# Routed expert tiles: turning the gathered rows by SBUF transfers and 32x32 blocks on VectorE in place of TensorE transposes

## The chip, the core and the metric

One core of one Trainium2 chip runs one program. The metric is device time in microseconds (us). The engines are called PE (TensorE; PEld is its weight load), DVE (VectorE), ACT (ScalarE), POOL (GpSimd) and SP (SyncE, which only issues transfers). A q behind a name (SPq) is that engine's instruction sequencer.

## The reference, cut to what matters

```
y      = clip((x * styles) @ weight.T * dcoefs + bias)       # 8192 tokens of 512 columns
shared = silu(y @ sh_gate_w) * (y @ sh_up_w) @ sh_down_w     # 1024 hidden
topk_idx, w = _route(y, router_w, e_bias)                    # 8 of 64 experts for each token
g = ragged_dot(y[tok], gate_w, group_sizes)                  # 512 -> 256 for each token's expert
u = ragged_dot(y[tok], up_w, group_sizes)
o = ragged_dot(silu(g) * u, down_w, group_sizes)             # 256 -> 512
out = x + shared + scatter_add(o * w)
```

Everything is float32. Each product is made of three fp32r matmuls: both operands are split in a high and a low part, and high by high, high by low and low by high are added up in PSUM.

## The kernel before, in words

**Dense stage (up to about 1396 us).** 16 blocks of 512 tokens: y is made in columns, turned back to rows and stored in `y_rows` in DRAM by `y_row` (line 624), the shared network is computed and stored in `out`, and the router writes for each expert a list of slots (row of y, weight) in `slot_list`. A table of tiles is made at the end: each tile has 128 rows of one expert.

**Routed stage (from about 1396 us).** 532 tiles of 128 rows (133 turns of `UN` = 4 tiles). Every engine runs its own `step(g, u)` for tile j = 4g + u in program order; semaphores join them:

- SP (lines 1101 to 1162): `step` of n loads tile n's list (`load_list`, line 1106; it waits until the scatter of tile n - 16 has landed, line 1112), and then, if tile n - 2 is the first one of an expert, loads that expert's weights (`weights`, line 1116): three transfers, 1.57 MB. `weights` waits until the weights before have landed (lines 1127, 1129). There are 29 such loads.
- POOL (from line 1164): `step(j)` waits until PE has turned tile j (`pe_x`, line 1190), gathers the 128 rows of tile j + 4 from `y_rows` into `x_rows` (line 1169), waits for `act_do`, reads a field of the table, and adds the result of tile j - 3 to `out` (`scatter`, line 1185). For a flagged tile (the first of an expert, and filling tiles) it first waits until all scatters before have landed.
- PE (from line 1214): `step(j)` is `gate_up(j)` (12 matmuls, line 1232), `turn_x(j + 2)` (4 transposes of the gathered rows into the PSUM banks `b_x`, line 1223), `turn_h(j - 1)` (2 transposes, line 1241), `down(j - 2)` (6 matmuls, line 1250).
- ACT (from line 1286): `weigh(j - 3)` (line 1315), `start_weights(j + 2)` if an expert begins there, `silu(j)` (line 1300), `x_high(j + 2)` (line 1294), `h_high(j - 1)`, `end_weights`.
- DVE (from line 1377): `weights_low` parts 1 and 2 of tile j + 1's expert if it begins there, `hidden(j)` (line 1398), `x_low(j + 2)`, `rows_from(j + 6)` (line 1387, the row numbers for the gather), `h_low(j - 1)`, `weights_low` part 0 of tile j + 2's expert. The subtractions all go through the helper `sub_exact` and so show line 30.

`gate_up(j)` waits for `x_low(j)`; `turn_h(j)` for `hidden(j)`; `down(j - 1)` for `h_low(j - 1)`; `hidden(j)` for `silu(j)`, and that for `gate_up(j)`. `weigh(j)` may write its buffer once the scatter of tile j - 4 has landed. `x_rows` has 4 buffers, `b_x` and `x_h`/`x_l` have 2.

The order of the experts puts a small one between two large ones: 9 times one tile of a small expert stands ahead of a large one, so that two loads of weights follow each other with one tile's list between them; twice two lists stand between the two loads, and the remaining 6 loads behind the first one of the stage lie further apart or close such a wider group.

Of the kernel before, what the change touches and what calls it, by code (L numbers as in the profile page):

```python
# [16 lines left out]
P = 128  # L17
# [15 lines left out]
def build(nc, x, cond, cw, cbias, aff_w, aff_b, router_w, e_bias, gate_w, up_w, down_w,  # L33
# [18 lines left out]
    UN = 4  # L52
# [4 lines left out]
    FLD = 7  # L57

# [11 lines left out]
    with top:  # L70
# [224 lines left out]
        with ExitStack() as tmp:  # L295
# [311 lines left out]
            def _(act):  # L607
# [16 lines left out]
                def y_row(q, t):  # L624
                    act.wait_ge(pe_ty, TT * q + t + 1)
                    if some(16 * (TT // 2 * q + t // 2)):
                        act.wait_ge(y_st[t % 2], 16 * (TT // 2 * q + t // 2))
                    nc.scalar.copy(yrow[:, t % 2, :], misc[(t + 1) % 2][:]).then_inc(act_yrow, 1)
# [391 lines left out]
        with ExitStack() as tmp:  # L1020
# [13 lines left out]
            xg = [sb(f"x_rows{n}", [P, C], F32, LINE) for n in range(UN)]  # L1034
            xp = [sb("x_h", [P, 2, KC, P], F32R, LINE), sb("x_l", [P, 2, KC, P], F32R, LINE)]
            sg = sb("e_sg", [P, 2, H])
            hf = sb("e_hf", [P, 2, H], F32, LINE)
            ident_r = sb("ident_r", [P, P], F32R, LINE)
# [3 lines left out]
            b_gu, b_x, b_h, b_o = bank[0:2], bank[2:4], bank[4:6], bank[6:8]  # L1042
# [10 lines left out]
            words, words_chain, ident_ok = sem("words"), sem("words_chain"), sem("ident_ok")  # L1053
            pe_x, act_x, dve_x = sem("pe_x"), sem("act_x"), sem("dve_x")
# [9 lines left out]
            AHEAD = 2  # L1064
# [37 lines left out]
            def _(sp):  # L1102
# [32 lines left out]

                def step(g, u):
                    n = g * UN + u
                    load_list(n, u, g)
                    if not isinstance(n, int) or n >= AHEAD:
                        weights(n - AHEAD)  # L1140

# [7 lines left out]
                with sp.Fori(LISTS // UN, NTURN + 1) as g:  # L1149
                    with sp.If(last_turn >= g - 1):  # L1150
                        for u in range(UN):
                            step(g, u)
                for u in range(2):
                    sp.wait_ge(list_ld[u], 16 * last_turn + 32)
                    sp.nop(nofuse=True)
                    sp.wait_ge(added[u], 16 * last_turn)
                    sp.nop(nofuse=True)
                    off = field(sp, UN * last_turn + 2 * UN + u, 0, LROWS - P)
                    sp.dma_start(entry(UN * last_turn + 2 * UN + u, 0, 2), slots[bass.ds(off, P), :]).then_inc(list_ld[u], 16)
                for u in range(UN):  # L1160
                    sp.wait_ge(list_ld[u], 16 * last_turn + (48 if u < 2 else 32))
# [3 lines left out]
            def _(pool):  # L1165
                def gather(g, u):
                    pool.wait_ge(dve_from, g * UN + u + 1)
                    pool.nop(nofuse=True)
                    nc.gpsimd.indirect_dma_start(xg[u][:], None, y_rows,  # L1169
# [18 lines left out]
                def step(g, u):  # L1188
                    j = g * UN + u
                    pool.wait_ge(pe_x, j + 1)  # L1190
                    gather(g + 1, u)
# [4 lines left out]
                for u in range(UN):  # L1196
                    gather(0, u)
# [11 lines left out]
                for u in range(UN):  # L1209
                    pool.wait_ge(x_ld[u], 16 * last_turn + 32)  # L1210
# [4 lines left out]
            def _(pe):  # L1215
                pe.wait_ge(tab_ld, 16)
                pe.sem_inc(pe_do, 1)

                def turn_x(j, u, g):

                    pe.wait_ge(x_ld[u], 16 * (g + 1))
                    for k in range(KC):
                        last = nc.tensor.transpose(b_x[u % 2][:, k * P:(k + 1) * P].bitcast(F32R),  # L1223
                                                   xg[u][:, k * P:(k + 1) * P].bitcast(F32R), ident_r[:])
                    last.then_inc(pe_x, 1)
# [29 lines left out]
                def step(g, u, turn):  # L1255
# [5 lines left out]
                    turn_x(j + 2, (u + 2) % UN, g + 1 if u >= UN - 2 else g)  # L1261
# [5 lines left out]
                pe.wait_ge(ident_ok, 1)  # L1267
                pe.wait_ge(words, 1)
                turn_x(0, 0, 0)
                turn_x(1, 1, 0)  # L1270
# [16 lines left out]
            def _(act):  # L1287
                act.wait_ge(tab_ld, 16)

                def x_high(j, u):  # L1290
                    act.wait_ge(pe_x, j + 1)
                    if not isinstance(j, int) or j >= 2:
                        act.wait_ge(pe_gu, j - 1)
                    nc.scalar.copy(xp[0][:, u % 2, :, :].rearrange("p k t -> p (k t)"), b_x[u % 2][:]).then_inc(act_x, 1)  # L1294
# [83 lines left out]
            def _(dve):  # L1378
                dve.wait_ge(tab_ld, 16)
                dve.sem_inc(split, SPLIT_0)  # L1380
                nc.vector.tensor_copy(ident_r[:], ident[:]).then_inc(ident_ok, 1)
# [118 lines left out]
```

## Time and profile before

| | us |
|---|---|
| median of 3 runs | 3939.05 |
| lowest, highest of the 3 | 3933.24, 15044.9 |
| the profiled execution's own time | 3924.35 |
| its span | 3922.7 |
| mean granted TensorE clock over the span | 0.988 |

The profile is of one execution. Its span runs from the first to the last instruction, and its own time is 1.65 us more than the span. Both are some 15 us (0.4%) below the median of the runs.

### The profile page before, as it was taken

How to read it: one execution, taken by the hardware profiler on the slowest of the kernel's cores; microseconds unless marked ns; L12 is line 12 of the kernel's file. 1: busy time of each engine (PE TensorE's matmuls, PEld its weight loads, DVE VectorE, ACT ScalarE, POOL GpSimd, SP SyncE). 2: the span in 40 equal slices, each digit the busy share in tenths (PEclk: the TensorE clock that was granted, in tenths of full speed). 3: DMA queues.
4: the chain of work that ended last, by engine and by line, in shares of the span. 5: the costliest groups of instructions: out<-in, count | busy, mean ns of one | idle time of the engine just before them, and what ended most of it. 6: DMA issues, size and time to landing. Idle time of an engine off the chain costs nothing.

```text
span 3922.7 us, 92670 instructions
## 1 busy us (share of the span) xinstructions
PE 3834.2 (98%) x19160; PEld 3179.8 (81%) x19161; DVE 1691.2 (43%) x4076; ACT 1507.8 (38%) x3339; POOL 1921.1 (49%) x1598
## 2 busy tenths in 40 slices
PE   6999999999999969999999999999999999999998
PEld 5888888888888858888888888888888888888886
DVE  4655555555555633333333333333333333333343
ACT  3222222222222224444444444444444444444444
POOL 1353343333343425555555555555555555555554
PEclk7999999999999989999999999999999999999999
DMA  5121121121122136666666676667676666777766
GB/s 183 44 66 44 44 59 51 49 60 44 50 61 44 33 88 113 113 139 120 113 144 115 114 144 113 143 115 145 113 144 113 144 144 113 145 144 145 146 144 128
DMA packets 296940, 409.20 MB, mean 104 GB/s; under 512 B 116137, under 2 KB 151345, under 8 KB 296817
## 3 DMA queue, kind: packets, MB, share of 16 engines
q0 software_dynamic: 135872, 280.60, 38.2%
q1 hardware_dynamic: 160946, 127.03, 12.3%
q8 instruction: 70, 1.15, 0.2%
q14 instruction: 52, 0.43, 0.1%
HBM read 228.29 MB, written 179.19 MB: 104 GB/s over the span
## 4 chain that ended last, share of the span: by engine, by line
PE 62%; issue 1%; DVE 0%; ACT 0%; ACTq 0%; DVEq 0%; SPq 0%; DMA 0%; POOL 0%; POOLq 0%
PE bank L1232 36%; PE bank L1250 18%; PE bank L1223 4%; PE bank L1241 3%; DVE w_dn_l L30 0%; ACTq L1068 0%; SPq L1068 0%; ACT w_dn_h L1320 0%; DVEq L1079 0%; DMA trow<-tile_table 0%; ACT w_gu_h L1320 0%; ACT x_h L1294 0%; DVE turns L1444 0%; DVE w_gu_l L30 0%; ACTq L1320 0%
## 5 line engine op out<-in xcount | busy, mean ns | idle before, releaser
L1185 POOL DMA_INDIRECT out_dram<-o_rows,to_row x532 | 862.0, 1620 | 930.6 <-issue 750.2
L425 POOL DMA_INDIRECT slot_list<-ent,pos x512 | 504.5, 985 | 822.3 <-PE bank L451 377.0
L1398 DVE TENSOR_TENSOR e_hf<-bank,e_sg 128x256 f32<-128x256 f32 x532 | 225.6, 424 | 1554.6 <-ACT e_sg L1300 1162.6
L1232 PE MATMUL bank<-w_gu_h,x_h 128*128 x2128 | 831.5, 391 | 10.1 <-DVE x_l L30 5.1
L1232 PE MATMUL bank<-w_gu_h,x_l 128*128 x2128 | 830.9, 390 | 0.0
L1232 PE MATMUL bank<-w_gu_l,x_h 128*128 x2128 | 828.9, 390 | 0.0
L1169 POOL DMA_INDIRECT x_rows<-y_rows,from_row x536 | 535.5, 999 | 213.3 <-issue 129.2
L1300 ACT ACTIVATE e_sg<-bank 128x256 f32<-128x256 f32 x532 | 204.4, 384 | 833.5 <-PE bank L1232 831.8
L1232 PEld LDWEIGHTS bank<-w_gu_h,x_h 128*128 128x128 f32 x2128 | 399.9, 188 | 102.1 <-issue 18.9
L1232 PEld LDWEIGHTS bank<-w_gu_h,x_l 128*128 128x128 f32 x2128 | 400.1, 188 | 83.5
L1232 PEld LDWEIGHTS bank<-w_gu_l,x_h 128*128 128x128 f32 x2128 | 400.0, 188 | 82.3
L1250 PE MATMUL bank<-w_dn_h,e_h_h 128*128 x1064 | 463.0, 435 | 0.5 <-issue 0.5
L1250 PE MATMUL bank<-w_dn_l,e_h_h 128*128 x1064 | 418.2, 393 | 0.0
L1250 PE MATMUL bank<-w_dn_h,e_h_l 128*128 x1064 | 414.8, 390 | 0.0
L30 DVE TENSOR_TENSOR x_l<-bank,x_h 128x512 fp32r<-128x512 f32 x534 | 368.9, 691 | 28.8
L1315 ACT ACTIVATE o_rows<-bank,lists 128x512 f32<-128x512 f32 x532 | 367.4, 691 | 0.0
L1223 PEld LDWEIGHTS bank<-ident_r,x_rows 128*128 128x128 f32 x2136 | 241.5, 141 | 95.0 <-issue 25.5
L1294 ACT CAST x_h<-bank 128x512 fp32r<-128x512 f32 x534 | 313.5, 587 | 0.0
L1314 ACT COPY to_row<-lists 128x1 int32 (+1 forms) x532 | 102.4, 192 | 519.2 <-PE bank L1250 510.5
L1223 PE MATMUL bank<-ident_r,x_rows 128*128 128x128 f32 x2136 | 246.0, 239 | 25.8 <-DVE turns L1450 24.9
L652 ACT ACTIVATE sg<-bank 128x512 f32<-128x512 f32 x128 | 76.6, 598 | 426.4 <-PE bank L451 426.4
L1250 PEld LDWEIGHTS bank<-w_dn_h,e_h_l 128*128 128x128 f32 x1064 | 200.5, 188 | 44.7
(244 smaller groups left out, 5988.9 us busy)
## 6 DMA issues: line engine op xcount, KB each, us to landing
xin<-in_x_dram SPq DMA_DIRECT2D x16, 1024.0 KB, 5.8
y_rows<-yrow SPq DMA_DIRECT2D x64, 256.0 KB, 3.1
stage_d<-in_x_dram SPq DMA_DIRECT2D x16, 1024.0 KB
out_dram<-stage_d SPq DMA_DIRECT2D x16, 1024.0 KB, 8.4
raw_gu<-in_L_ffn_gate_w_dram SPq DMA_DIRECT2D x29, 512.0 KB
raw_gu<-in_L_ffn_up_w_dram SPq DMA_DIRECT2D x29, 512.0 KB
raw_d<-in_L_ffn_down_w_dram SPq DMA_DIRECT2D x29, 512.0 KB
lists<-slot_list SPq DMA_DIRECT2D x538, 1.0 KB
```

The lines of the kernel that those rows point to most:

```text
L30: return nc.vector.tensor_tensor(out, full, high.bitcast(F32), ALU.subtract)
L425: nc.gpsimd.indirect_dma_start(slots, bass.IndirectOffsetOnAxis(ap=pos[v][:, t, k:k + 1], axis=0), ent[v][:, t, k, :], None).then_inc(scat ...
L1169: nc.gpsimd.indirect_dma_start(xg[u][:], None, y_rows, bass.IndirectOffsetOnAxis(ap=from_row[u][:].bitcast(U32), axis=0)).then_inc(x_ld[u] ...
L1185: nc.gpsimd.indirect_dma_start(out, bass.IndirectOffsetOnAxis(ap=to_row[u][:].bitcast(U32), axis=0), og[u][:], None, compute_op=ALU.add).t ...
L1223: last = nc.tensor.transpose(b_x[u % 2][:, k * P:(k + 1) * P].bitcast(F32R), xg[u][:, k * P:(k + 1) * P].bitcast(F32R), ident_r[:])
L1232: last = nc.tensor.matmul(b_gu[u % 2][:], xp[a][:, u % 2, k, :], wgu[b][:, bass.ds(place, 1), k, :].rearrange("p a n -> p (a n)"), start=( ...
L1241: last = nc.tensor.transpose(b_h[u % 2][:, k * P:(k + 1) * P], hf[:, u % 2, k * P:(k + 1) * P], ident[:])
L1250: last = nc.tensor.matmul(b_o[u % 2][:], hp[a][:, u % 2, k, :], wdn[b][:, bass.ds(place, 1), k, :].rearrange("p a n -> p (a n)"), start=(k ...
L1294: nc.scalar.copy(xp[0][:, u % 2, :, :].rearrange("p k t -> p (k t)"), b_x[u % 2][:]).then_inc(act_x, 1)
L1300: nc.scalar.activation(sg[:, u % 2, :], b_gu[u % 2][:, 0:H], ACT.Silu).then_inc(act_gu, 1)
L1315: nc.scalar.activation(og[u][:], b_o[u % 2][:], ACT.Copy, scale=entry(j, 1, 2).bitcast(F32)).then_inc(act_do, 1)
L1398: nc.vector.tensor_tensor(hf[:, u % 2, :], b_gu[u % 2][:, H:2 * H], sg[:, u % 2, :], ALU.mult).then_inc(dve_gu, 1)
```

## The change

`turn_x` leaves PE. The gathered rows take another way into columns:

- `y_row` stores each row of y with its 512 columns in another order: column 128m + 32a + r goes to place 128a + 32m + r. The rest of the dense stage is as before.
- SP gets `spread(j)`: once the gather of tile j has landed and DVE has turned tile j - 2, four transfers inside SBUF bring quarter a of the 128 rows (128 partitions of 512 bytes) to the 32 partitions from 32a on (2048 bytes each) of `x_split`, which has 2 buffers.
- DVE gets `turn_x(j)`: one 32x32 block transpose of 128x512 elements from `x_split` into the new SBUF tile `x_cols`.
- `x_high` and `x_low` read `x_cols` in SBUF instead of the PSUM bank `b_x`.
- The gathers run two tiles further ahead (tile j + 6 in POOL's step j, ahead of it a wait for the spread of tile j + 2 in place of the wait for `pe_x`), `rows_from` one tile further, DVE's `turn_x` stands one tile ahead of `x_low`. SP's loop runs one turn longer, in place of the two list loads behind it.

```diff
@@ y_row
-                    nc.scalar.copy(yrow[:, t % 2, :], misc[(t + 1) % 2][:]).then_inc(act_yrow, 1)
+                    nc.scalar.copy(yrow[:, t % 2, :].rearrange("p (a m r) -> p m a r", a=QD, m=KC),
+                                   misc[(t + 1) % 2][:].rearrange("p (m a r) -> p m a r", m=KC, a=QD)).then_inc(act_yrow, 1)
@@ tiles
+            x_split = [sb(f"x_split{n}", [P, QD, KC * SQ]) for n in range(2)]
+            x_cols = sb("x_cols", [P, 2, KC, P])
-            ident_r = sb("ident_r", [P, P], F32R, LINE)
-            AHEAD = 2
+            AHEAD, BEHIND = 2, 5
@@ SP
+                def spread(j, u, g):
+
+                    sp.wait_ge(x_ld[u], 16 * (g + 1))
+                    sp.nop(nofuse=True)
+                    if not isinstance(j, int) or j >= 2:
+                        sp.wait_ge(dve_turned, j - 1)
+                        sp.nop(nofuse=True)
+                    for a in range(QD):
+                        sp.dma_start(x_split[u % 2][a * SQ:(a + 1) * SQ, :, :],
+                                     xg[u][:, a * P:(a + 1) * P]).then_inc(x_moved[u], 16)
+
                 def step(g, u):
                     n = g * UN + u
                     load_list(n, u, g)
+                    if not isinstance(n, int) or n >= BEHIND:
+                        spread(n - BEHIND, (u - BEHIND) % UN, g + (u - BEHIND) // UN)
                     if not isinstance(n, int) or n >= AHEAD:
                         weights(n - AHEAD)
-                with sp.Fori(LISTS // UN, NTURN + 1) as g:
-                    with sp.If(last_turn >= g - 1):
+                with sp.Fori(LISTS // UN, NTURN + 2) as g:
+                    with sp.If(last_turn >= g - 2):
@@ POOL
                 def gather(g, u):
                     pool.wait_ge(dve_from, g * UN + u + 1)
                     pool.nop(nofuse=True)
+                    if some(g):
+                        pool.wait_ge(x_moved[u], 16 * QD * g)
+                        pool.nop(nofuse=True)
@@ POOL step
-                    pool.wait_ge(pe_x, j + 1)
-                    gather(g + 1, u)
+                    gather(g + 1 + (u + 2) // UN, (u + 2) % UN)
@@ PE
-                def turn_x(j, u, g):
-
-                    pe.wait_ge(x_ld[u], 16 * (g + 1))
-                    for k in range(KC):
-                        last = nc.tensor.transpose(b_x[u % 2][:, k * P:(k + 1) * P].bitcast(F32R),
-                                                   xg[u][:, k * P:(k + 1) * P].bitcast(F32R), ident_r[:])
-                    last.then_inc(pe_x, 1)
@@ PE step
                     gate_up(j, u, place)
-                    turn_x(j + 2, (u + 2) % UN, g + 1 if u >= UN - 2 else g)
@@ ACT x_high
-                    act.wait_ge(pe_x, j + 1)
+                    act.wait_ge(dve_turned, j + 1)
-                    nc.scalar.copy(xp[0][:, u % 2, :, :].rearrange("p k t -> p (k t)"), b_x[u % 2][:]).then_inc(act_x, 1)
+                    nc.scalar.copy(xp[0][:, u % 2, :, :], x_cols[:, u % 2, :, :]).then_inc(act_x, 1)
@@ DVE
-                    sub_exact(nc, xp[1][:, u % 2, :, :].rearrange("p k t -> p (k t)"), b_x[u % 2][:],
-                              xp[0][:, u % 2, :, :].rearrange("p k t -> p (k t)")).then_inc(dve_x, 1)
+                    sub_exact(nc, xp[1][:, u % 2, :, :], x_cols[:, u % 2, :, :], xp[0][:, u % 2, :, :]).then_inc(dve_x, 1)
+
+                def turn_x(j, u, g):
+                    dve.wait_ge(x_moved[u], 16 * QD * (g + 1))
+                    if not isinstance(j, int) or j >= 2:
+                        dve.wait_ge(act_x, j - 1)
+                        dve.wait_ge(dve_x, j - 1)
+                    nc.vector.transpose(x_cols[:, u % 2, :, :].rearrange("p k (c i) -> p k i c", i=QD),
+                                        x_split[u % 2][:].rearrange("p i (k r) -> p k i r", r=SQ)).then_inc(dve_turned, 1)
@@ DVE step
                     hidden(j, u)
+                    turn_x(j + 3, (u + 3) % UN, g + (u + 3) // UN)
                     x_low(j + 2, (u + 2) % UN)
-                    rows_from(j + 2 + UN, (u + 2) % UN, g + 2 if u >= UN - 2 else g + 1)
+                    rows_from(j + 3 + UN, (u + 3) % UN, g + 1 + (u + 3) // UN)
@@ DVE ahead of the loop
+                for u in range(3):
+                    rows_from(UN + u, u, 1)
+                for u in range(2):
+                    turn_x(u, u, 0)
                 for u in range(2):
                     x_low(u, u)
-                    rows_from(UN + u, u, 1)
+                turn_x(2, 2, 0)
```

## Rows read from the trace of the kernel before

**Rows 1.** The page's chain that ended last, shares of the span by line.

```profile
PE bank L1232 36%; PE bank L1250 18%; PE bank L1223 4%; PE bank L1241 3%; DVE w_dn_l L30 0%; ACTq L1068 0%; SPq L1068 0%; ACT w_dn_h L1320 0%; DVEq L1079 0%; DMA trow<-tile_table 0%; ACT w_gu_h L1320 0%; ACT x_h L1294 0%; DVE turns L1444 0%; DVE w_gu_l L30 0%; ACTq L1320 0%
```

**Rows 2.** Windows: length; busy PE, PEld, DVE, ACT, POOL (count); PE clock; DMA share; GB/s.

```profile
1400.00:1425.00 25.00, 6.21 (x19) 4.91 (x20) 8.75 (x20) 3.91 (x5) 5.73 (x6) 0.50 0.45 127
1420.00:3923.00 2503.00, 2479.90 (x12768) 2062.70 (x12768) 892.92 (x2214) 1121.74 (x2744) 1393.67 (x1064) 1.00 0.67 129
```

**Rows 3.** Timeline of one tile: start us, length us, engine, line, what.

```profile
2401.15 0.39 PE L1232 MATMUL bank<-w_gu_h,x_h 128*128 x1
...
2401.76 0.69 ACT L1315 ACTIVATE o_rows<-bank,lists 128x512 f32<-128x512 f32 x1
...
2403.88 0.46 PE L1223 MATMUL bank<-ident_r,x_rows 128*128 128x128 f32 x4
2404.03 1.59 POOL L1185 DMA_INDIRECT out_dram<-o_rows,to_row  x1 [1.88 <-issue]
...
2404.17 0.41 PE L1241 MATMUL bank<-ident,e_hf 128*128 128x128 f32 x2
2404.33 0.48 PE L1250 MATMUL bank<-w_dn_h,e_h_h 128*128 x1
...
2404.99 0.69 DVE L30 TENSOR_TENSOR x_l<-bank,x_h 128x512 fp32r<-128x512 f32 x1
...
2405.66 0.41 DVE L30 TENSOR_TENSOR e_h_l<-bank,e_h_h 128x256 fp32r<-128x256 f32 x1
2405.80 0.39 PE L1232 MATMUL bank<-w_gu_h,x_h 128*128 x1
2405.93 0.98 POOL L1169 DMA_INDIRECT x_rows<-y_rows,from_row  x1 [0.30 <-DVE from_row L1387]
```

**Rows 4.** Timeline of SP where two loads of weights follow each other.

```profile
2502.59 0.34 SPq L1114 DMA_DIRECT2D lists<-slot_list  x1
2506.32 0.40 SPq L1131 DMA_DIRECT2D raw_gu<-in_L_ffn_gate_w_dram  x1
...
2507.51 0.38 SPq L1133 DMA_DIRECT2D raw_d<-in_L_ffn_down_w_dram  x1
2509.17 0.36 SPq L1114 DMA_DIRECT2D lists<-slot_list  x1
2515.73 0.40 SPq L1131 DMA_DIRECT2D raw_gu<-in_L_ffn_gate_w_dram  x1
```

**Rows 5.** Waits of SP in 2500 to 2520: us in total, times, longest.

```profile
SPq L1129 <- DMA raw_d<-in_L_ffn_down_w_dram: 3.1, 1, 3.1
```

**Rows 6.** SP's issues and table reads, all of them: ns min/median/max.

```profile
L1114 SPq DMA_DIRECT2D lists<-slot_list x536: 345/351/369, 1403.8 to 3862.1; - x179
L1131 SPq DMA_DIRECT2D raw_gu<-in_L_ffn_gate_w_dram x29: 392/403/423, 1401.5 to 3859.1; - x29
L1068 SPq TENSOR_LOAD <-trow x1131: 260/268/1018, 1399.0 to 3888.3; - x189
```

**Rows 7.** Windows, ahead of a load of weights and in it (columns as in rows 2).

```profile
2490.00:2506.00 16.00, 16.00 (x83) 13.31 (x82) 4.51 (x12) 6.39 (x16) 8.14 (x7) 1.00 0.68 115
2507.60:2515.20 7.60, 7.60 (x38) 6.29 (x38) 2.06 (x7) 2.77 (x7) 3.65 (x4) 1.00 1.03 297
```

**Rows 8.** The page's queue of SP's transfers: packets, MB, share of 16 engines.

```profile
q1 hardware_dynamic: 160946, 127.03, 12.3%
```

**Rows 9.** Groups of DVE and its release of PE, 1500 to 3850 and 1450 to 3890.

```profile
L30 DVE TENSOR_TENSOR w_gu_l<-raw_gu,w_gu_h x52 | 61.6, 1219 | 3.6 <-issue 3.3
L30 DVE TENSOR_TENSOR w_dn_l<-raw_d,w_dn_h x26 | 31.6, 1216 | 0.0
PE bank L1232 <- DVE w_dn_l L30: 3.9, 9, 0.6
```

**Rows 10.** Timeline: POOL beside DVE's work on weights, and POOL when it is late.

```profile
1729.69 1.22 DVE L30 TENSOR_TENSOR w_dn_l<-raw_d,w_dn_h  x1
...
1730.23 2.15 POOL L1185 DMA_INDIRECT out_dram<-o_rows,to_row  x1 [2.96 <-PE bank L1223]
...
1764.72 0.98 POOL L1169 DMA_INDIRECT x_rows<-y_rows,from_row  x1 [0.30 <-issue]
1766.01 1.59 POOL L1185 DMA_INDIRECT out_dram<-o_rows,to_row  x1 [0.30 <-issue]
...
1769.19 1.59 POOL L1185 DMA_INDIRECT out_dram<-o_rows,to_row  x1 [0.30 <-issue]
```

More of the change, by code:

```diff
@@ L57, in build @@
     FLD = 7
+    SQ = 32
+    QD = P // SQ
+    assert KC * SQ == P
     xf = x.rearrange("b l c -> (b l) c")
@@ L1037, in build @@
             hf = sb("e_hf", [P, 2, H], F32, LINE)
-            ident_r = sb("ident_r", [P, P], F32R, LINE)
             hp = [sb("e_h_h", [P, 2, KH, P], F32R, LINE), sb("e_h_l", [P, 2, KH, P], F32R, LINE)]
             og = [sb(f"o_rows{n}", [P, C]) for n in range(UN)]
-            b_gu, b_x, b_h, b_o = bank[0:2], bank[2:4], bank[4:6], bank[6:8]
+            b_gu, b_h, b_o = bank[0:2], bank[4:6], bank[6:8]
             tab_ld = sem("tab_ld")
@@ L1052, in build @@
             w_high = sem("w_high")
-            words, words_chain, ident_ok = sem("words"), sem("words_chain"), sem("ident_ok")
-            pe_x, act_x, dve_x = sem("pe_x"), sem("act_x"), sem("dve_x")
+            words, words_chain = sem("words"), sem("words_chain")
+            x_moved = [sem(f"x_moved{n}") for n in range(UN)]
+            dve_turned, act_x, dve_x = sem("dve_turned"), sem("act_x"), sem("dve_x")
             pe_gu, act_gu, dve_gu = sem("pe_gu"), sem("act_gu"), sem("dve_gu")
@@ L1148, in _ @@
                 last_turn = field(sp, 0, 5, NTURN - 1)
-                with sp.Fori(LISTS // UN, NTURN + 1) as g:
-                    with sp.If(last_turn >= g - 1):
+                with sp.Fori(LISTS // UN, NTURN + 2) as g:
+                    with sp.If(last_turn >= g - 2):
                         for u in range(UN):
                             step(g, u)
[L1153 to L1159, printed above, removed]
                 for u in range(UN):
-                    sp.wait_ge(list_ld[u], 16 * last_turn + (48 if u < 2 else 32))
+                    sp.wait_ge(list_ld[u], 16 * last_turn + 48)
                     sp.nop(nofuse=True)
@@ L1195, in _ @@
                 pool.wait_ge(tab_ld, 16)
-                for u in range(UN):
-                    gather(0, u)
+                for n in range(UN + 2):
+                    gather(n // UN, n % UN)
                 for u in range(UN):
@@ L1209, in _ @@
                 for u in range(UN):
-                    pool.wait_ge(x_ld[u], 16 * last_turn + 32)
+                    pool.wait_ge(x_ld[u], 16 * last_turn + (48 if u < 2 else 32))
                 for u in range(UN):
@@ L1265, in step @@
                         down(j - 2, (u - 2) % UN, turn.place(u - 2))
-                pe.wait_ge(ident_ok, 1)
                 pe.wait_ge(words, 1)
-                turn_x(0, 0, 0)
-                turn_x(1, 1, 0)
                 for g in range(2):
```

1 line of the change is left out of this document (removed).

## The prediction

> **What bounds the kernel now.** I read the chain that ended last first. PE's lines make nearly all of it, and the transposes of the gathered rows (L1223) have 4% of the span, some 157 us [rows 1]. The window over the routed stage then says that PE is busy 2479.90 of 2503 us at clock 1.00, with DVE at 893, ACT at 1122 and POOL at 1394 us [rows 2]. The timeline of one tile gives the pace: `gate_up` starts at 2401.15 and the next one at 2405.80, so 4.65 us a tile without a gap: 2.73 for the 12 matmuls, 0.29 for `turn_x` (2403.88 to 2404.17), 0.16 for `turn_h`, 1.47 for `down` [rows 3]. PE is the bound, and what comes off it counts only until something else is late. So the other readings are of the engines and the queue that take the work over: SP's timeline at a load of weights [rows 4, 5], the cost of SP's instructions [rows 6], the DMA share in such a load [rows 7], and the groups and the timeline of DVE and POOL [rows 9, 10].
>
> **The change part by part.** I sum against the profiled execution (span 3922.7 us, own time 3924.35); the median of the runs is 3939.05, 15 us more, and I carry the difference over to it.
>
> *PE.* 532 times 0.29 us: -154 us. That is the row's gap between two starts and not the 0.46 us of busy time. The new pace would be 4.36 us.
>
> *DVE, in an ordinary tile.* It gets one transpose of 128x512 more. No row shows one. Below, the subtraction of the same shape takes 0.69 us [rows 3]; above, I take twice that, 1.38, if it goes at half rate. I take 0.69. `x_low` from SBUF I cost at nothing: `w_dn_l`, with all operands in SBUF, takes 1.216 us for 1024 elements a partition [rows 9], which lies on one line with 0.69 for 512. The deadline: `gate_up`'s last matmul ends at about 2404.03 and `h_low(j - 1)` at 2406.07, 2.04 later, 2.8 with the transpose. `down(j - 1)`, which needs it, would start at 2404.33 - 0.29 + 4.36, 4.4 later [rows 3]. 1.5 us are left, so nothing is paid. At 1.38 there are 0.8 left, and still nothing is.
>
> *DVE, where an expert begins.* `weights_low` adds 2 times 1.22 and 1.22, 3.65 us [rows 9]. Now PE waits 9 times for `w_dn_l`, 3.9 us in all [rows 9], at the 9 places where two loads follow each other: there DVE is just late. At these, two or three transposes more (1.4 to 2.1 us) meet a PE that is 0.6 to 0.9 us earlier: about 2.2 us each, +20 us. From both sides: 0, if ACT's and DVE's start moves ahead, and 45 us with transposes of 1.38.
>
> *ACT.* `x_high` reads SBUF instead of PSUM; `silu` and `h_high` stay as they are. 0, with 0.05 us each way, hidden as ACT is busy 45% [rows 2]. The copy in `y_row` moves the same 512 elements in runs of 32; its 64 copies lie beside a PE-bound dense stage: 0.
>
> *SP.* Its step has two table reads (0.268 each and as much again around them), one issue (0.351) and waits [rows 6]. From the end of the weights' last issue (2507.89) to the start of the next list's issue are 1.28 us, and from a list's issue to the first issue of weights, with three reads on the way, 3.73 [rows 4]. I work out 2.3 to 2.4 us for an ordinary step (1.28 + 0.35 + one read and its branch at 0.7). `spread` adds two waits with their nops (0.25) and four issues. Each lasts between 0.351 (one row of descriptors a partition) and 0.403 (the weights' shape) [rows 6], 0.04 between them: 1.6 to 1.8. The new step is 4.2 to 4.4 us, and I take 4.3: just under PE's 4.36. SP becomes the second bound, which is a rival below. A step with weights is 6.58 (2502.59 to 2509.17) [rows 4], 4.25 more than an ordinary one.
>
> *The spread's way through the queue.* 256 KB a tile in pieces of 512 bytes. No row shows a transfer inside SBUF. Queue q1's mean packet costs 0.123 * 3922.7 * 16 / 160946 = 48 ns for 789 bytes [rows 8]: by bytes 1.0 us a tile on all 16 engines, by packets 1.5. DMA share would go from 0.67 to 0.67 * 4.65 / 4.36 + 1.0 / 4.36 = 0.94 (1.06 by packets, which would be too much; 0.71 if it cost nothing). I take 1.0: bytes, since both sides lie in SBUF. In an ordinary tile it is in time. Call T the moment at which DVE has turned tile k - 2 and `spread(k)` may be issued. It is 1.65 us behind the end of `gate_up(k - 5)`, as the transpose takes the place of today's `x_low` (2404.99) and lasts 0.69; DVE wants tile k 0.95 us behind the end of `gate_up(k - 3)`, which is T + 8.0, and PE feels it at T + 9.5. Issues until T + 1.8 and a landing some 3 us later leave 4 us: nothing is paid.
>
> *Behind a load of weights* it is paid. The weights go through the same queue as the spreads. A load issued from 2506.32 on has landed at 2515.4 (SP waited 3.1 us for it, up to just ahead of 2515.73), 9.1 us, with the DMA engines at 1.03 [rows 4, 5, 7]. In the new order SP issues `spread(a - 3)` and then the weights of tile a. By its step costs the first of these goes out at T + 1.8 + 3.4, T + 5.2, and the load lands at T + 14.3. `spread(a - 2)`, issued from T + 8 on, stands behind it: T + 16 (1.3 us at the rate of 1.57 MB in 7.6 us, and its receipt), wanted by T + 4.4 + 9.5 = T + 13.9. PE loses 2.2 us. Where the next tile begins an expert too, SP waits for that landing, issues the second load from T + 14.5 on, and `spread(a - 1)` after it lands behind it, at T + 14.5 + 9.1 + 1 + 1.6 = T + 26.2, wanted by T + 8.7 + 9.5 + 2.2 = T + 20.4: 5.8 us more, 8.3 with some jitter. The tile after that is in time. So: 9 close pairs at 8.3 are 75 us, the two wider ones at 5 are 10, 6 other loads at 2.2 are 13: +98 us. From both sides: 0, if transfers don't keep this order, and 160, if the spread goes by packets and half of the stalls are 5 us longer.
>
> *POOL.* Its step ahead of `gather` swaps one wait for another under the scatter (1.59 us), so 0 by itself. Now act_do (end of 2401.76 + 0.69) leads to a scatter 1.58 us later, the scatter and its 0.31 to the next gather, and that ends at 2406.91: 4.46 us [rows 3], more than 4.36. But that isn't a floor. When POOL is late, it repeats each 3.18 us (1766.01 to 1769.19), since it then reads its table under the transfer before [rows 10]. So it falls back by about 1 us and stays there; gathers run a step earlier than needed. Cost 0; from above, the rival.
>
> The trace shows what two SBUF operands on DVE do to POOL: the scatter that starts under `w_dn_l` takes 2.15 instead of 1.59 us [rows 10], about as long as that instruction still ran. `x_low` becomes such an instruction, 0.69 us in each tile: 3.18 + 0.69 = 3.9 us, still under 4.36, so 0. (The Trainium skill, page SBUF — State Buffer, section "SBUF: two separate sides", says that GpSimd shares a port pair with VectorE as an exclusive lock, taken by a VectorE operation in a 2-port mode or with two SBUF inputs. It speaks against moving operands from PSUM to SBUF; the trace agrees for two inputs, and nothing here shows a transpose.)
>
> *Start and end.* Ahead of the first `gate_up` DVE does two transposes and three `rows_from`: +2 us. After the last tile nothing is new.
>
> Sum: -154 + 98 + 20 + 2 = -34 us. From 3924.35 that is 3890, and from the median of 3939 it is **3905 us**, ratio 0.991.
>
> **The rivals.**
>
> *SP is the bound (slower).* SP's chain has its own sum: 532 steps, 29 times 4.25 for weights (123) and 9 times 2 for landings (18). PE's is 532 * 4.36 + 120 = 2440 and that of before 532 * 4.65 = 2474. With a step of 4.3 SP's is 2429 and hidden; from 4.43 on it equals that of before; at 4.6 it is 2588, +114: 4053 us. For it: 4.3 stands on two estimates, and each 0.1 us in the step is 53 us. The table reads go up to 1.018 us [rows 6]. Against it: the issue times are narrow.
>
> *The queue keeps nobody waiting (faster).* If a spread overtakes a load, or lands in time, only 20 + 2 stay: 3939 - 132 = 3807; with the DVE term gone too, 3787. For it: the packets of two queues share the engines, and 4 us of slack are there. Against it: the same queue holds both, and the engines were full for 7.6 us [rows 7].
>
> *POOL is the bound.* If the transpose also shuts POOL out, its step is 3.18 + 1.38 = 4.56 when it meets both: 532 * 4.56 + some 40 for flagged tiles less 2474 is -8: 3931 us.
>
> *The clock.* PE's clock was at 0.50, its level of 1.2 GHz, after 20 us without work, and the first `gate_up` paid some 2.5 us [rows 2]. If each stall of 6 us does that, it is 9 * 2.5, 22 us more: 3927, inside the forecast's own range.
>
> **How the numbers follow.** Forecast with the clock's variant 0.48, queue harmless 0.17, SP 0.23, POOL 0.12. What this measurement can tell from no change is about 2%, so 3860 and 4018. Faster: 0.16 of the second and 0.04 of the first case, 0.20. Slower: 0.20 of SP's and 0.04 of forecast and POOL, 0.24. Same: 0.56. The range takes in the harmless queue and SP at 4.6: 3790 to 4055; the forecast's own is 3850 to 3960.
>
> **What would show it.** Right: the gap between two `gate_up` starts is 4.36 us in the middle of a large expert; PE idles ahead of `down` or `gate_up`, released by DVE's `e_h_l`, some 2 us at each load of weights and 6 at the second one of a close pair, about ten tiles ahead of the expert's first; DVE waits there for the DMA of `x_split`; the transpose lasts 0.69; DMA share is near 0.94. Wrong: SP is never waiting in an ordinary tile and the pace is 4.5 or more; or PE's idle time is under 40 us in all; or POOL's transfers grow beyond 4 us a tile.

## The result and the profile after

The changed kernel takes 4421.07 us (median of 4, 4418.56 to 4432.33), the kernel before 3936.14 beside it: ratio 1.1254, 95% interval 1.1221 to 1.1287. The ratio leaves out the one run of the kernel before that took 15044.9 us, and it isn't the quotient of the two medians, which is 1.123. The forecast was 3905 us and its range ended at 4055. The direction is that of the rival "SP is the bound", and the size is about four times its price of 114 us.

The page after, in this order: busy time by engine, the queue of the hardware transfers, the chain that ended last by engine and by line, and the groups of the new transpose, of the casts and subtractions behind it, and of POOL.

```profile
PE 3841.4 (87%) x17024; PEld 3058.4 (69%) x17025; DVE 2166.1 (49%) x4611; ACT 1526.4 (35%) x3339; POOL 1947.0 (44%) x1600
...
q1 hardware_dynamic: 469394, 267.42, 21.9%
...
SPq 52%; issue 14%; DMA 2%; PE 0%; POOLq 0%; DVE 0%; POOL 0%; DVEq 0%; ACT 0%; ACTq 0%
SPq L1150 28%; SPq L1074 15%; SPq L1120 6%; DMA raw_d<-in_L_ffn_down_w_dram 1%; SPq L1137 1%; SPq L1124 1%; SPq L1147 0%; SPq L1168 0%; DMA x_split<-x_rows 0%; SPq L1118 0%; SPq L1139 0%; DMA out_dram<-o_rows,to_row 0%; SPq L1145 0%; SPq L1148 0%; SPq L1117 0%
...
L1399 DVE STREAM_TRANSPOSE x_cols<-x_split 128x512 f32<-128x512 f32 x535 | 585.4, 1094 | 1057.0 <-DMA x_split<-x_rows 1056.2
...
L1200 POOL DMA_INDIRECT out_dram<-o_rows,to_row x532 | 868.8, 1633 | 386.7 <-issue 372.6
...
L30 DVE TENSOR_TENSOR x_l<-x_cols,x_h 128x512 fp32r<-128x512 f32 x534 | 359.3, 673 | 0.2 <-ACT x_h L1296 0.2
```

Before, PE's lines made the chain [rows 1]. Now 52% of the span is SP's sequencer: 28% the four issues of `spread` (L1150), 15% the reads of the table (L1074), 6% the issue of the lists (L1120). PE has 0%.

The window over the routed stage (columns as in rows 2) answers to [rows 2]:

```profile
1420.00:4419.00 2999.00, 2493.15 (x10640) 1945.79 (x10640) 1365.53 (x2746) 1140.02 (x2744) 1416.49 (x1064) 0.96 0.76 155
```

It is 496 us longer than the stage of before, and no engine is full: PE idles 506 us. Who waits, over 1450 to 4400 us (us in total, times, longest), and the only row that this view has for SP:

```profile
DVE x_cols L1399 <- DMA x_split<-x_rows: 1044.3, 463, 9.7
...
PE bank L1256 <- DVE e_h_l L30: 404.3, 224, 7.8
```

```profile
SPq L1135 <- DMA raw_d<-in_L_ffn_down_w_dram: 2.9, 4, 1.0
```

DVE waits for the spread in 463 tiles, PE for DVE in 224, and SP for next to nothing: 2.9 us in 2950. A queue that never waits, while the engines that need what it issues do, is the likely bound; the experiments below test it. SP's instructions (ns min/median/max, first and last start), and its timeline at the pair of loads of [rows 4]:

```profile
L1150 SPq DMA_DIRECT2D x_split<-x_rows x2140: 556/595/1327, 1408.8 to 4390.3; - x195
```

```profile
L1074 SPq TENSOR_LOAD <-trow x1137: 261/277/1137, 1394.5 to 4391.0; - x190
```

```profile
2501.89 0.35 SPq L1120 DMA_DIRECT2D lists<-slot_list  x1
2502.46 2.57 SPq L1150 DMA_DIRECT2D x_split<-x_rows  x4
2506.95 0.35 SPq L1120 DMA_DIRECT2D lists<-slot_list  x1
2507.52 2.52 SPq L1150 DMA_DIRECT2D x_split<-x_rows  x4
```

An issue of `spread` takes 595 ns, not the 351 to 403 of the issues of before [rows 6], and four of them 2.5 to 2.6 us (mean 2.53), from one start to the next 0.64 to 0.66. The step's mean is (4390.3 - 1408.8) / 535 = 5.57 us; 2.53 of it are the four issues, 3.04 the rest. The starts of two `gate_up` on PE are 5.60 apart in the mean: PE goes at SP's pace.

### The profile page after: what moved, and what is told of

Same layout as the page of the kernel before. It is cut to its first block, busy times and chain, and to the rows that moved or that the text cites. A ratio compares the mean times of both kernels' runs of the same rounds, so it can differ in the third digit from the quotient of the medians.

```text
span 4419.7 us, 93909 instructions
## 1 busy us (share of the span) xinstructions
PE 3841.4 (87%) x17024; PEld 3058.4 (69%) x17025; DVE 2166.1 (49%) x4611; ACT 1526.4 (35%) x3339; POOL 1947.0 (44%) x1600
## 4 chain that ended last, share of the span: by engine, by line
SPq 52%; issue 14%; DMA 2%; PE 0%; POOLq 0%; DVE 0%; POOL 0%; DVEq 0%; ACT 0%; ACTq 0%
SPq L1150 28%; SPq L1074 15%; SPq L1120 6%; DMA raw_d<-in_L_ffn_down_w_dram 1%; SPq L1137 1%; SPq L1124 1%; SPq L1147 0%; SPq L1168 0%; DMA x_split<-x_rows 0%; SPq L1118 0%; SPq L1139 0%; DMA out_dram<-o_rows,to_row 0%; SPq L1145 0%; SPq L1148 0%; SPq L1117 0%
## 5 line engine op out<-in xcount | busy, mean ns | idle before, releaser
L1399 DVE STREAM_TRANSPOSE x_cols<-x_split 128x512 f32<-128x512 f32 x535 | 585.4, 1094 | 1057.0 <-DMA x_split<-x_rows 1056.2
L1184 POOL DMA_INDIRECT x_rows<-y_rows,from_row x538 | 553.6, 1029 | 1233.5 <-DVE from_row L1388 1092.6
L1238 PE MATMUL bank<-w_gu_h,x_h 128*128 x2128 | 865.2, 407 | 115.4 <-issue 45.0
L1238 PE MATMUL bank<-w_gu_l,x_h 128*128 x2128 | 846.9, 398 | 0.0
L1256 PE MATMUL bank<-w_dn_h,e_h_h 128*128 x1064 | 480.2, 451 | 409.6 <-DVE e_h_l L30 404.3
L1256 PEld LDWEIGHTS bank<-w_dn_h,e_h_h 128*128 128x128 f32 x1064 | 205.3, 193 | 494.2 <-issue 468.7
L1256 PE MATMUL bank<-w_dn_h,e_h_l 128*128 x1064 | 434.8, 409 | 0.0
L1296 ACT CAST x_h<-x_cols 128x512 fp32r<-128x512 f32 x534 | 327.6, 614 | 130.8 <-DVE x_cols L1399 128.9
L30 DVE TENSOR_TENSOR x_l<-x_cols,x_h 128x512 fp32r<-128x512 f32 x534 | 359.3, 673 | 0.2 <-ACT x_h L1296 0.2
L1256 PEld LDWEIGHTS bank<-w_dn_l,e_h_h 128*128 128x128 f32 x1064 | 208.5, 196 | 25.9
```

The source lines that it names most:

```text
L30: return nc.vector.tensor_tensor(out, full, high.bitcast(F32), ALU.subtract)
L1184: nc.gpsimd.indirect_dma_start(xg[u][:], None, y_rows, bass.IndirectOffsetOnAxis(ap=from_row[u][:].bitcast(U32), axis=0)).then_inc(x_ld[u] ...
L1238: last = nc.tensor.matmul(b_gu[u % 2][:], xp[a][:, u % 2, k, :], wgu[b][:, bass.ds(place, 1), k, :].rearrange("p a n -> p (a n)"), start=( ...
L1256: last = nc.tensor.matmul(b_o[u % 2][:], hp[a][:, u % 2, k, :], wdn[b][:, bass.ds(place, 1), k, :].rearrange("p a n -> p (a n)"), start=(k ...
L1296: nc.scalar.copy(xp[0][:, u % 2, :, :], x_cols[:, u % 2, :, :]).then_inc(act_x, 1)
L1399: nc.vector.transpose(x_cols[:, u % 2, :, :].rearrange("p k (c i) -> p k i c", i=QD), x_split[u % 2][:].rearrange("p i (k r) -> p k i r", ...
```

## The experiments

Ratios are to the kernel before, timed on the same chip, so they compare across chips and the microseconds less well. The median of the kernel before was 3924.5 beside idle_on_before, half_bytes, two_on_act and words_on_sp, 3960.8 beside idle_flat, act_and_words, weights_in_pieces and idle_turn, and 3960.9 beside the rest. The microseconds that were expected were worked out for the first of these chips. "Period" is the time between two tiles' copies of `to_row` on ACT.

### Is it the instructions on SP?

**idle_on_before.** The kernel before, with `spread`'s four transfers issued into a buffer that nobody reads, and a wait for the transfers of two tiles back. PE still does the transposes.

```diff
+                def idle_spread(j, u, g):
+                    if not isinstance(j, int) or j >= 2:
+                        sp.wait_ge(idle_moved[(u - 2) % UN], 64 * (g + 1 if u >= 2 else g))
+                        sp.nop(nofuse=True)
+                    for a in range(4):
+                        sp.dma_start(idle_to[u % 2][a * 32:(a + 1) * 32, :, :],
+                                     zrow[:, a * P:(a + 1) * P]).then_inc(idle_moved[u], 16)
@@ step
                     load_list(n, u, g)
+                    idle_spread(n, u, g)
```

> The kernel before, to which SP's step gets only the four issues of the change: the same shapes inside SBUF, from a constant tile into a tile that nobody reads, so that no engine waits for them; PE still turns the rows. Theory 1 (the changed kernel is bound by SP's instructions: 5.59 us a tile in its trace, 2.58 of them the four issues): SP's step is 5.3 to 5.6 us here too, the lists come late, and the time is 4300 to 4420 us. Theory 2 (the transfers themselves are late, in the queue or on full DMA engines, and DVE waits for their data): nobody waits for them here, so the time stays under 3980 us. Theory 3 (the DVE transpose and its ports): no transpose here, 3935 us.

Measured: 4372.0 us, ratio 1.1132 (1.1081 to 1.1184), +448 us of the change's +485. The issue, the chain, and who waits longest over 1450 to 4300 us (us in total, times, longest):

```profile
L1143 SPq DMA_DIRECT2D idle_to<-zrow x2144: 547/602/1163, 1400.5 to 4327.9; - x195
```

```profile
SPq 53%; issue 14%; DMA 2%; DVEq 0%; PE 0%; DVE 0%; POOL 0%; POOLq 0%; ACT 0%; ACTq 0%
SPq L1143 29%; SPq L1070 15%; SPq L1116 6%; DMA raw_d<-in_L_ffn_down_w_dram 1%; SPq L1133 1%; SPq L1120 1%; SPq L1161 0%; SPq L1114 0%; SPq L1135 0%; SPq L1140 0%; DMA lists<-slot_list 0%; SPq L1141 0%; SPq L1162 0%; SPq L1113 0%; SPq L1111 0%
```

```profile
DVE from_row L1402 <- DMA lists<-slot_list: 1044.1, 397, 13.6
```

The chain has the shares of the changed kernel's, though no engine waits for these transfers. What is late behind them are the lists, which SP issues too: DVE waits for them 1044.1 us. The loss is SP's time, not the way of the rows.

**half_bytes.** The change, with each transfer moving 256 bytes of each 512 (half of the gathered columns are left out; the rest of `x_split` is zero, by two clears on DVE at the stage's begin).

```diff
-                        sp.dma_start(x_split[u % 2][a * SQ:(a + 1) * SQ, :, :],
-                                     xg[u][:, a * P:(a + 1) * P]).then_inc(x_moved[u], 16)
+                        sp.dma_start(x_split[u % 2][a * SQ:(a + 1) * SQ, :, 0:P // 2],
+                                     xg[u][:, a * P:a * P + P // 2]).then_inc(x_moved[u], 16)
```

> The changed kernel, each of the four transfers with rows of 256 instead of 512 bytes: as many issues and rows, half the bytes. It leaves out half of each gathered row (zeros in its place). Theory 1 (SP's issues): 4390 to 4430 us, no change. Theory 2 (bytes on the DMA engines or in the queue): the share of the DMA engines falls by about a tenth of the span, and the time by over 100 us, to under 4320.

Measured: 4391.67 us, ratio 1.1183, an issue still 595 ns. Half the bytes give back 0.7%, some 28 us, and the intervals of the two ratios (1.1126 to 1.1239 here) overlap. Bytes are not the main cause.

**idle_flat.** As idle_on_before, but from 128 partitions to the same 128 partitions: no change of shape.

```diff
-                        sp.dma_start(idle_to[u % 2][a * 32:(a + 1) * 32, :, :],
+                        sp.dma_start(idle_to[u % 2][:, a, :],
                                      zrow[:, a * P:(a + 1) * P]).then_inc(idle_moved[u], 16)
```

> As idle_on_before, but each of SP's four idle transfers goes from 128 partitions straight to the same 128 partitions (512 bytes each) instead of to 32 of them: as many issues and bytes. If the 0.6 us of an issue come from the change of shape (128 rows into 32 partitions of 4), the issues take 0.35 to 0.40, SP's step is 4.5 to 4.7 us, and the time 3930 to 4020 us. If each transfer inside SBUF costs SP 0.6 us, it is 4350 to 4380 as in idle_on_before.

Measured: 4441.48 us, ratio 1.1201; an issue has a median of 601 ns. The spreading over quadrants is not what makes the issue dear.

**pairs_of_tiles.** Each of the four transfers carries two tiles: half as many issues of `spread` on SP, as many bytes in as many pieces. (To make room the fourth buffer of `o_rows` is the tile of zeros, and the table is read in shorter.)

```diff
-            x_split = [sb(f"x_split{n}", [P, QD, KC * SQ]) for n in range(2)]
+            x_split = [sb(f"x_split{n}", [P, QD, 2, KC * SQ]) for n in range(2)]
@@ spread, in each second step only
                     for a in range(QD):
-                        sp.dma_start(x_split[u % 2][a * SQ:(a + 1) * SQ, :, :],
-                                     xg[u][:, a * P:(a + 1) * P]).then_inc(x_moved[u], 16)
+                        sp.dma_start(x_split[u // 2][a * SQ:(a + 1) * SQ, :, :, :],
+                                     xg2[u // 2][:, :, a * P:(a + 1) * P]).then_inc(x_moved[u // 2], 16)
```

> The four transfers carry two tiles each: as many bytes and pieces as in the change, half as many instructions on SP. Theory 'price per instruction' (0.644 us from one start to the next, whatever it carries): 1.29 us per tile beside 3.01 of the rest, an SP step of 4.3 us, just under PE's 4.37: period median 4.35 to 4.5, ratio to before 1.01 to 1.04. Theory 'price per piece or byte': an issue takes some 1.2 us, the step stays near 5.6 us and the ratio near 1.12.

Measured: 4107.94 us, ratio 1.036 (1.0337 to 1.0383), period median 4.47. Its page, SP's issues (ns min/median/max) and its timeline:

```profile
x_split<-x_rows SPq DMA_DIRECT2D x1072, 128.0 KB
```

```profile
L1152 SPq DMA_DIRECT2D x_split<-x_rows x1072: 17/631/1659, 1438.6 to 4083.8; - x179
```

```profile
2600.92 0.35 SPq L1121 DMA_DIRECT2D lists<-slot_list  x1
2601.79 2.67 SPq L1152 DMA_DIRECT2D x_split<-x_rows  x4
```

Four issues of 128 KB take 2.67 us where four of 64 KB took 2.57: the price is per instruction. It gives back some 350 of the 485 us. The spread now also waits for two gathers, so each pair comes later, and SP itself waits 111.9 us for `x_rows`.

### What taking work off SP is worth

**two_on_act.** Two of the four transfers are issued by ACT, which gets the same two waits ahead of them.

```diff
-                    for a in range(QD):
+                    for a in range(QD // 2):
                         sp.dma_start(...)
@@ ACT, at the start of its step
+                    for a in range(QD // 2, QD):
+                        act.dma_start(x_split[u % 2][a * SQ:(a + 1) * SQ, :, :],
+                                      xg[u][:, a * P:(a + 1) * P]).then_inc(x_moved[u], 16)
```

> The changed kernel, two of the four transfers issued by ACT instead of SP. Same bytes, same shapes, same 16 DMA engines. Theory 1: SP's step falls by half of 2.58 us to 4.3, just under PE's 4.36; what is left is stalls of some 100 us at the loads of weights, so 3900 to 4000 us. ACT has some 2.3 us of work a tile and gets 1.3 more, with no harm. Theory 2: the transfers are as late as before, over 4300 us.

Measured: 4016.56 us, ratio 1.0227 (1.018 to 1.0274), with act_and_words below the best of the change's variants that compute the whole result. The period's median is 4.37, and from one `gate_up` to the next it is 4.35: the pace of 4.36 that the forecast gave PE is real once SP is out of the way. The mean is 4.835: some tiles are far longer.

**words_on_sp.** SP reads a packed word of four tiles where it read the table for each (lists excepted), and the weights go two tiles earlier.

```diff
-                    with sp.If(field(sp, j, 3, 1) > 0):
+                    with sp.If((field(sp, j, 3, 1) if first is None else first) > 0):
@@ step
-                    if not isinstance(n, int) or n >= AHEAD:
-                        weights(n - AHEAD)
+                    if turn is not None:
+                        weights(n, turn.first(u))
```

> The changed kernel, SP learns from a packed word once in four tiles whether an expert begins, as the other engines do, instead of by one table read in each tile. No transfer changes, weights are loaded two tiles earlier. Theory 1: a table read with its register work is 0.75 us of SP's step, less 0.15 for the word, so the step is 5.0 and the time 4080 to 4150 us. Theories 2 and 3: no change, 4400 to 4430 us.

Measured: 4246.78 us, ratio 1.0814, period median 4.96: 534 of SP's 1137 reads are gone and with them 4.4%, some 170 us, where 270 to 340 were expected. By the mean of SP's step, 5.23 us for 5.57, a read and its branch less the word's share are worth 0.34, where I had 0.6.

**act_and_words** has both.

> Both of the reliefs for SP at once: two of the four transfers issued by ACT, and the packed word instead of the table read. SP's step is then some 3.7 us, clear of PE's 4.36. Theory A (what is left at the loads of weights is the queue: spreads wait behind 1.57 MB): the stalls at the loads stay, the time is 3930 to 4000 us, near that of two_on_act. Theory B (what is left is still SP, which falls behind by 4 us in a step with weights and makes it up slowly): the stalls shrink by half, under 3900 us.

Measured: 4061.15 us, ratio 1.0242 (1.0198 to 1.0287), median 4.38, mean 4.836: as two_on_act. SP now waits 259.7 us for DVE (over 1450 to 4000 us):

```profile
SPq L1149 <- DVE x_cols L1423: 259.7, 246, 3.8
```

So SP's time is not what two_on_act still loses; that lies elsewhere.

**pairs_and_words** puts the words on pairs_of_tiles.

> The same with SP's own table reads for the weights taken from a packed word, and the weights two tiles earlier: an SP step of some 3.9 us. If SP is what pairs_of_tiles still loses by, the ratio falls to 1.00 to 1.01; if it is the stalls at the loads of weights (two_on_act and act_and_words stood at 1.023 and 1.024), it stays between 1.01 and 1.03.

Measured: 4068.61 us, ratio 1.0273 (1.0246 to 1.03): three ways of freeing SP end between 1.023 and 1.027.

### What is left once SP is free

SP's timeline in two_on_act at a close pair of loads, and the window on the first of them (columns as in rows 2):

```profile
1686.83 1.23 SPq L1150 DMA_DIRECT2D x_split<-x_rows  x2
1690.82 0.41 SPq L1137 DMA_DIRECT2D raw_gu<-in_L_ffn_gate_w_dram  x1
...
1694.12 1.38 SPq L1150 DMA_DIRECT2D x_split<-x_rows  x2
1700.59 0.39 SPq L1137 DMA_DIRECT2D raw_gu<-in_L_ffn_gate_w_dram  x1
...
1703.93 1.30 SPq L1150 DMA_DIRECT2D x_split<-x_rows  x2
```

```profile
1691.00:1701.00 10.00, 9.29 (x44) 7.35 (x42) 2.76 (x6) 3.53 (x9) 5.16 (x5) 1.00 1.01 267
```

The spreads there are 7.3 and 9.8 us apart instead of 4.4, with the DMA engines at 1.01; two periods of 10.5 and 7.0 us follow at 1695 and 1705. Where these experts' weights are then split on DVE, three more of 6.7, 7.1 and 5.8. I sorted all 531 periods of two_on_act by what lies in them and summed what each is above the median: 100 us in the 47 in which DVE starts a subtraction of weights, 137 us in some 60 others at loads or just behind one, 10 us in the rest. (The kernel before has 8, -7 and -43 us.) Some periods belong to both kinds; with those counted as loads it is 90 and 148.

Part of this is PE's clock. In two_on_act, from 1475 us on, it was at 0.50, its level of 1.2 GHz, in 21 stretches of 139 us in all, behind waits of PE; in the kernel before in 2 of 18 us. The 201 matmuls in these stretches are some 0.2 us further apart each, as the last section shows for six of them: an estimate of 40 us, more than the 22 of the forecast's variant "the clock".

**weights_in_pieces.** act_and_words with an expert's three transfers of weights in three steps, so that spreads go between them.

```diff
-                        weights(n, turn.first(u))
+                        if not isinstance(n, int) or n > UN:
+                            piece(n - 1, turn.first(u - 1), 2)
+                        piece(n, turn.first(u), 1)
+                        piece(n + 1, turn.first(u + 1), 0)
```

> As act_and_words, and SP issues an expert's three weight transfers in three steps, one tile apart, instead of in one step. Theory A (spreads wait behind the weights in SP's queue): no spread has more than 0.5 to 1.0 MB ahead of it, so the periods of over 10 us at close pairs of experts go, and the time falls to 3850 to 3920 us. Theory C (the engines are full in these stretches, whatever the order): the same bytes, so within 20 us of act_and_words.

Measured: 4118.56 us, ratio 1.0387: worse by 57 us, where 140 to 210 less were expected. The periods at a pair are 11.8 and 8.2 us. The order in the queue alone is not the cause. The bytes are the same, and SP's steps have more reads and waits; that these make the stalls grow is not shown.

**light_before** and **light_two_on_act.** Each of an expert's three transfers of weights a quarter as wide, the rest of the raw weights zero: three quarters of the weights' bytes are left out, no issue is.

```diff
-                            sp.dma_start(raw[0][:, bass.ds(half, 1), :, n * H:(n + 1) * H]...
+                            sp.dma_start(raw[0][:, bass.ds(half, 1), :, n * H:n * H + H // 4]...
@@ and down_w to 0:C // 4; two clears of raw on DVE at the stage's begin
```

> Control: the kernel before with each of an expert's three transfers of weights a quarter as wide (the rest of the raw weights is zero from the start; two clears of the raw weights at the stage's begin, some 10 us). The kernel before lost little at the loads (sum over median 30 us): 3915 to 3950, ratio 0.99 to 1.005, if weights cost nothing but their place; the clears are in it.

> two_on_act with the same light weights. Theory 'queue and engines at the loads': most of its 90 us over before goes, 3930 to 3970, within 1% of light_before, and the periods of 10 to 13 us before an expert are gone. Theory 'VectorE and ScalarE where an expert begins': the periods of 6.7, 7.1 and 5.8 us stay and with them a ratio of 1.015 to 1.025 to light_before.

Measured: 3971.75 us, ratio 1.0032 (1.0015 to 1.005), for light_before, and 3998.58 us, ratio 1.0086 (1.0064 to 1.0108), for light_two_on_act: 27 us between the two, where the full weights leave two_on_act some 90 over before. In the sorted periods, the part at loads falls from 137 to 78 us and the part at DVE's subtractions stays (100 and 98). So 59 us of the stalls are the weights' bytes. Some 38 of what stays are again PE at 0.50 (189 matmuls in 22 stretches, an estimate as above). And SP's steps that hold weights are still long: at 1741.04 and 1748.87 two spreads are 7.8 us apart. That last is a reading of the timeline; no run took those steps away:

```profile
1741.04 0.88 SPq L1151 DMA_DIRECT2D x_split<-x_rows  x2
1745.29 0.39 SPq L1138 DMA_DIRECT2D raw_gu<-in_L_ffn_gate_w_dram  x1
...
1748.87 1.20 SPq L1151 DMA_DIRECT2D x_split<-x_rows  x2
```

DVE's timeline in light_two_on_act where an expert begins:

```profile
1764.62 1.10 DVE L1421 STREAM_TRANSPOSE x_cols<-x_split 128x512 f32<-128x512 f32 x1
1765.57 0.68 DVE L30 TENSOR_TENSOR x_l<-x_cols,x_h 128x512 fp32r<-128x512 f32 x1
...
1766.55 2.35 DVE L30 TENSOR_TENSOR w_gu_l<-raw_gu,w_gu_h  x2
1768.81 1.22 DVE L30 TENSOR_TENSOR w_dn_l<-raw_d,w_dn_h  x1
1771.10 0.42 DVE L1428 TENSOR_TENSOR e_hf<-bank,e_sg 128x256 f32<-128x256 f32 x1 [1.07 <-ACT e_sg L1315]
1771.44 1.14 DVE L1421 STREAM_TRANSPOSE x_cols<-x_split 128x512 f32<-128x512 f32 x1
```

From transpose to transpose 6.8 us, of which DVE is busy all but 1.07: in such a tile DVE's work sets the pace.

**idle_turn.** The kernel before with the change's transpose alone on DVE, from a buffer of zeros into one that nobody reads.

```diff
                     hidden(j, u)
+                    if not isinstance(j, int) or j >= 2:
+                        dve.wait_ge(idle_turned, j - 1)
+                    nc.vector.transpose(idle_cols[:, u % 2, :, :].rearrange("p k (c i) -> p k i c", i=4),
+                                        zrow[:].rearrange("p (i k r) -> p k i r", i=4, r=32)).then_inc(idle_turned, 1)
                     x_low(j + 2, (u + 2) % UN)
```

> The kernel before, to which DVE gets one transpose of the change's size and patterns in each tile, from a constant tile into one that nobody reads; no transfers. The cost of DVE's part alone: in ordinary tiles hidden (1.09 us in 3 us of idle time), and paid where an expert begins: PE's waits for w_dn_l grow from 3.9 us to 30 to 50, time 3940 to 3985 us. If POOL is shut out while DVE transposes: its transfers grow from 1.62 and 1.00 us by over 0.2 on the mean, and the time goes over 4000.

Measured: 3980.7 us, ratio 1.0054 (1.0034 to 1.0075), some 20 us. PE's waits for DVE's subtractions of weights, over 1450 to 3900 us, beside 3.9 us in 9 of before [rows 9]:

```profile
PE bank L1234 <- DVE w_dn_l L30: 18.1, 23, 1.0
```

## Why the prediction was wrong, step by step

**The step that failed** is the one on SP: "Each lasts between 0.351 (one row of descriptors a partition) and 0.403 (the weights' shape) [rows 6], 0.04 between them: 1.6 to 1.8." The four issues take 2.53, each 0.60. So SP's step is 5.57 and not 4.3, and SP, not PE, is the bound. I priced a transfer inside SBUF by the issues of transfers that have DRAM on one side, though the next part says itself that no row shows a transfer inside SBUF; there I bounded its bytes from both sides, and here not its issue. The working around it holds in the main. With 2.6 for the rest of an ordinary step and 2.53 the step is 5.13, and the rival's own sum gives 532 * 5.13 + 141 = 2870, +396 us; the span grew by 497. The remainder, 0.19 a tile, is the rest of the step: 3.04 in the mean where my terms give 2.6, 0.23 for weights and 0.03 for landings. The table reads have a part in it: their mean is 0.36 us where it was 0.31, two a tile, though their median went only from 0.268 to 0.277.

**The rival** "SP is the bound" was right in place and mechanism and wrong in price: its end, 4.6 us, still used the same issue time. It deserved an upper bound such as twice the dearest issue shown, 0.8 us; that gives a step of 5.9 and would have held the result. Its threshold was wrong too: SP's sum equals the 2474 of before at a step of 4.39, not 4.43. "Against it: the issue times are narrow" was no argument, since all narrow rows were of other kinds of transfer.

**PE, -154.** Right in size: the median from one `gate_up` to the next is 4.35 in two_on_act, for 4.36.

**Behind a load of weights, +98.** Right in mechanism, short in size: 137 us at loads in two_on_act, 59 of which go with three quarters of the bytes. In the changed kernel no run tells it apart from SP's own lateness.

**DVE where an expert begins, +20.** The size depends on the pace. At the old pace the transpose alone costs 20 us (13 to 30 by the interval) and makes PE's waits 14 us longer (idle_turn). At 4.37 it is some 100: a tile with 3.57 us of weights keeps DVE at work for 6.8 us, as one timeline shows. I had counted only the 9 places where PE already waited; with a faster PE the 100 us lie in 47 tiles, and at the close pair shown in three of them.

**DVE in an ordinary tile.** 1.09 us, inside the bounds and above the 0.69 I took; it was to cost nothing up to 1.38, and the median of 4.37 bears that out. `x_low` from SBUF costs 0.67 for 0.69.

**DMA share.** 0.94 was said for a pace of 4.36; it is 0.76 at 5.6 and 0.88 in two_on_act (1420 to 3950 us) at a mean of 4.84. By q1's rows [rows 8 and above] the change adds 0.219 * 4419.7 - 0.123 * 3922.7 = 485 us of the 16 engines, 0.91 us a tile: the 1.0 by bytes that I took, not the 1.5 by packets.

**POOL.** No bound: the scatter has a mean of 1.63 us, and 1.62 before (over 1450 to 3900 us). The forecast had two questions, and both have an answer. The transpose doesn't hold POOL up: in idle_turn 34 scatters and 117 gathers start under it, and none is longer than 1.60 and 0.99 us; in the changed kernel 118 scatters start under it and ahead of `x_low`, and none is longer than 1.61. The subtraction `x_low`, now with both operands in SBUF, does hold POOL up when it is under way first, as the forecast said: in the changed kernel 26 scatters start under it (with over 0.1 us of it left) and take 1.94 us in the mean, in two_on_act 256 and 1.86. One of idle_turn, and one of the changed kernel:

```profile
1777.22 1.08 DVE L1425 STREAM_TRANSPOSE idle_cols<-zrow 128x512 f32<-128x512 f32 x1
1777.50 1.59 POOL L1187 DMA_INDIRECT out_dram<-o_rows,to_row  x1 [2.90 <-PE bank L1225]
```

```profile
2619.75 0.67 DVE L30 TENSOR_TENSOR x_l<-x_cols,x_h 128x512 fp32r<-128x512 f32 x1
2619.89 1.99 POOL L1200 DMA_INDIRECT out_dram<-o_rows,to_row  x1 [1.35 <-issue]
```

Where POOL starts first its length stays as it was: of the 93 scatters into which a transpose ran in the changed kernel none is longer than 1.61 us. The mean of all scatters in two_on_act is 1.74 us; no PE wait there is put down to it.

**What this says of the idea.** With SP freed, the change brings PE's 154 us and gives back 247 at loads, at experts' starts and in the rest (137 + 100 + 10), some 90 net in two_on_act. Even with light weights it is 27 us behind the kernel before with light weights. No version that I ran beats the kernel before.

## What to carry to other kernels

Count the instructions of the queue that issues the transfers as you count an engine's, and ask of each price whether the row it comes from is the same kind of transfer; a kind with no row needs a wide upper bound, and a queue within a few per cent of the pace turns that bound into the forecast. A queue that never waits, while others wait for what it issues, is the first suspect, whatever the engines' shares say: look for the missing wait first. (The Trainium skill, page Perfetto Trace Analysis, section "What 'DMA-bound' means", names this second way of being bound: the sequencer that issues the transfers is solid with them. The trace agrees in part: SP waits 2.9 us in 2950, but issues are only about half of its step, 2.53 and 0.35 of 5.57 us, and the rest is table reads and what goes with them. The page's remedy is large descriptors; here the pieces stayed at 512 bytes, and halving the number of instructions took the ratio from 1.125 to 1.036.) Where the issues are the bound, carrying more in each helps (1.036) and carrying less hardly does (1.118); and slack counted at the old pace is not there at the new one.

## What the runs showed of the hardware that was not expected

- A transfer with both sides in SBUF costs SP 0.60 us to issue by the medians, whether it spreads over partitions (595, 602 ns) or not (601), and with 32 KB (595), 64 KB (595) or 128 KB (631). Issues with DRAM on one side have medians of 0.33 to 0.41, in the changed kernel too. Two kinds of its dense stage (ns min/median/max):

```profile
L376 SPq DMA_DIRECT2D y_rows<-yrow x64: 332/333/372, 61.0 to 1280.7; - x64
```

```profile
L390 SPq DMA_DIRECT2D out_dram<-stage_d x16: 372/383/383, 154.1 to 1385.8; - x16
```

  Neither SBUF as the source (both rows) nor 256 KB (the first) does it alone. Why both sides together do it is open.
- DVE's transpose of 128x512 in squares of 32 takes 1.09 us where a subtraction of the same shape takes 0.67.
- PE's clock can fall after a short wait too. PE waited 2.48 us up to 2506.08; the window behind it and the next (columns as in rows 2) read:

```profile
2506.05:2508.75 2.70, 2.67 (x6) 2.15 (x7) 2.01 (x4) 0.00 (x0) 2.18 (x2) 0.50 0.31 90
2509.10:2511.60 2.50, 2.50 (x12) 2.02 (x11) 0.00 (x0) 0.81 (x2) 1.03 (x2) 1.00 0.93 129
```

  At 0.50, its level of 1.2 GHz, six matmuls of `down` go 0.43 us apart instead of 0.23, 1.2 us more. After so short a wait it is the exception: from 1450 us on PE stands still 25 times for 2 to 3 us, and the clock is low behind 2 of them; it is low behind all 17 stops of over 5 us. There are 43 such stretches, 240 us in all, and the stage's mean clock is 0.96. The forecast allowed for one in each of 9 stalls. What they cost in the changed kernel, where SP is the bound, is not shown.
